# AdaLN/FFN adapter kernel on one core: two products with a narrow adapter matrix in two fp32r passes, hi and lo parts of the stationary operand side by side

## The chip, the cores and the metric

One Trainium2 chip, one of its cores. The metric is the device time of one execution in microseconds (us). TensorE's clock has two levels, 2.4 and 1.2 GHz; the profile gives the granted one as a share of full speed (1.0 or 0.5). Engines in the profile: PE is TensorE (PEld its weight loads), DVE VectorE, ACT ScalarE, POOL GpSimd, SP SyncE.

## What is computed

x has 8 batches of 256 tokens with 1024 features. The reference, cut to what matters:

```python
q     = quantize(x)             # 8 threshold groups: each element takes the step and zero point of its group
gates = softmax(top2(q @ router_w.T))                       # 4 experts
x1    = x + sum_e gates_e * (q @ A_e.T) @ B_e.T * 4         # rank 16 each, E*R0 = 64 in all
base  = x1 @ W.T + (x1 @ lora_A[label]) @ lora_B_w.T * 0.5  # rank 32, A chosen per batch
out   = x1 + base @ K + bias + (base @ A_eff.T) @ B_eff.T + (base @ A_s.T) @ B_s.T   # rank 32 each
```

## The kernel before

No product with W and then K is done per token. The kernel first forms K' = K + A_s.T B_s and P = W.T K' + I (1024 x 1024), and then out = x P + small terms. All products that need fp32 precision with large operands are done in fp32r passes: an operand is split into a hi part (a copy with rounding to fp32r, on ScalarE) and a lo part (the difference, on VectorE); three passes (hi hi, hi lo, lo hi) make one product. A matmul of plain fp32 operands shows as two records in the trace.

Stages, in order of time. (1) 0 to 36 us: loads; `aefft` (effective A of each batch), `k_update` and `k_add` form K' of the first half of the columns (`kst`, 8 tiles of 128x512); `kp_split` (ScalarE) and `kp_lo_part` (VectorE) split it into `kp_hi` and `kp_lo`. `keep_warm` issues matmuls whose result nobody reads. (2) `v_product(0)`: v = lora_B_w.T times K', 8 fp32 matmuls with the tile `bw` (lora_B_w tiled 4 times to 128 columns) as the stationary operand; `v_rows` copies 32 rows of it, times 0.5, into `tst`. (3) The T products: 8 fp32 matmuls (`gm` times `lb`, L828), which give the effective B of the batches; `rows_out` (ScalarE, L474) copies each into `tst`, which has two slots, and SyncE stores each slot to `t_dram` (L315). A slot is written again only when its store has landed (the wait on `t_stored`). (4) Steps 0 to 15 (`STEPS`), each one tile of P (128x512): steps 0 to 7 for the first half of K's columns, with the product u (L885, copied by ScalarE as `ust`, L523; the next u waits for that copy), steps 8 to 15 for the second half. Each is 24 passes (L902, L903, L906) of W's tile, split by `weight_hi` (ScalarE) and `weight_lo` (VectorE), with K'; its result is split into `p_hi` and `p_lo`. K' of the second half is made beside steps 0 to 7, split after step 7, and `v_product(1)` stands after step 7. (5) `bp`: the expert matrix B (`bet`, E*R0 = 64 columns, twice) times P: 48 passes, copied into the lower 64 rows of `tb` for both slots by `bp_out`. (6) 64 slots, 8 for each batch: x P in three passes (L949 to L951), `z_begin` and `z_end` (the adapter rows z, with `bu`), `close` (adapter rows times `tb`, L931), `out_tile` (bias, VectorE).

Beside all this ScalarE and VectorE quantize the batches: 64 groups `quant(c, g)` (batch c, group g), each two ScalarE passes over 2048 elements (L392, L403) and three VectorE ones (L576, L586, L593), and after the eighth group of a batch `finish` (L598), on which the `mid` products of TensorE (L837) wait. The order on every engine is written out by hand: the list `TAKEN` says how many groups stand in each slot; ScalarE is one slot ahead of VectorE. Every engine takes its instructions in order, and `wait_ge` holds the whole engine.

SyncE's order ahead of step 0: the 8 `alt` loads, the wait for kp_hi, kp_lo and v, the load of K's second half (`kst`, L311, 2 MB), then the four stores of `tst`.

## Time and profile before

| | us |
|---|---|
| median of 3 runs (lowest, highest) | 492.47 (491.3, 493.65) |
| span of the profiled execution, first to last instruction | 490.6 |
| its own time | not listed apart from the three runs; the lowest lies 0.7, the highest 3.05 above its span |
| TensorE busy | 471.1 |
| VectorE busy | 408.6 |
| ScalarE busy | 339.7 |
| mean granted clock of TensorE | 0.965 |

Times in the trace are us from the start of the span. A pair "start, us" is the start and the length of an instruction; a bracket behind it is the idle time of the engine just before and what ended it. A busy TensorE is not TensorE at its peak, since the ends of matmuls overlap: the pitch of two following records says what one costs.

### The profile page before, as it was taken

The numbers are of one execution on the slowest core, as the hardware profiler recorded it, in microseconds if no ns is written. First come the engines' busy times: TensorE is split into PE (matmuls) and PEld (weight loads), VectorE is DVE, ScalarE is ACT, GpSimd is POOL, SyncE is SP. The second block draws the span as 40 slices with busy tenths as digits, with TensorE's granted clock in tenths as the row PEclk, the third lists the DMA queues.
The fourth block names the chain that finished last, engine by engine and source line by source line (L and its number), as shares of the span: only waits on it lengthen the run. The fifth ranks groups of instructions, "written<-read, shape, count | busy, mean of one in ns | idle before, by whom it ended". The sixth has DMA issues, their size and how long they took to land.

```text
span 490.6 us, 5581 instructions
## 1 busy us (share of the span) xinstructions
PE 471.1 (96%) x2168; PEld 365.4 (74%) x2168; DVE 408.6 (83%) x411; ACT 339.7 (69%) x264; POOL 8.5 (2%) x12
## 2 busy tenths in 40 slices
PE   6989999999989999999999999999999989999796
PEld 5963888887758888787777777877787768767674
DVE  2289979779979989749899999999999994999402
ACT  3779987864978396676599596955977975583000
POOL 0000000001000000000000010000000000000000
PEclk9599999999999999999999999999999995999699
DMA  8975643212401527030523117104313130101102
GB/s 277 421 258 192 171 133 89 73 43 98 107 1 63 152 85 215 15 94 23 169 99 106 59 40 236 53 1 150 140 28 124 54 128 1 53 1 43 44 0 85
DMA packets 35499, 50.61 MB, mean 103 GB/s; under 512 B 26610, under 2 KB 26866, under 8 KB 33074
## 3 DMA queue, kind: packets, MB, share of 16 engines
q1 hardware_dynamic: 34322, 41.87, 26.6%
q0 software_dynamic: 1152, 8.39, 4.8%
q8 instruction: 17, 0.28, 0.2%
q14 instruction: 8, 0.07, 0.1%
HBM read 39.51 MB, written 10.49 MB: 102 GB/s over the span
## 4 chain that ended last, share of the span: by engine, by line
PE 62%; DVE 26%; issue 7%; DMA 2%; ACT 2%; SPq 0%; DVEq 0%; ACTq 0%
DVE val L593 12%; PE bank L949 7%; PE bank L951 7%; PE bank L950 7%; PE bank L837 6%; DVE val L576 5%; PE bank L906 5%; PE bank L902 5%; PE bank L903 4%; PE bank L931 3%; PE bank L863 3%; DVE inside L586 3%; PE bank L885 3%; PE bank L803 3%; DMA la<-la_in 2%
## 5 line engine op out<-in xcount | busy, mean ns | idle before, releaser
L403 ACT ACTIVATE val<-level,shift,small 128x2048 f32<-128x2048 int16 x64 | 133.8, 2090 | 22.5 <-DVE val L593 22.4
L593 DVE COPY_PREDICATED val<-inside,val 128x2048 f32<-128x2048 uint8 x56 | 142.1, 2538 | 0.3
L392 ACT ACTIVATE level<-xq,inv 128x2048 int16<-128x2048 f32 x64 | 127.9, 1998 | 2.2 <-DMA xq<-xt_in 1.4
L949 PE MATMUL bank<-p_hi,x_hi 128*128 128x512 f32 x256 | 113.1, 442 | 0.0
L951 PE MATMUL bank<-p_hi,x_lo 128*128 128x512 f32 x256 | 101.3, 396 | 0.0
L950 PE MATMUL bank<-p_lo,x_hi 128*128 128x512 f32 x256 | 101.2, 395 | 0.0
L576 DVE TENSOR_SCALAR val<-val,width,unshift 128x2048 f32<-128x2048 f32 x64 | 86.8, 1359 | 10.2 <-ACT val L403 10.0
L586 DVE TENSOR_SCALAR inside<-absx,thr 128x2048 uint8<-128x2048 f32 x56 | 72.1, 1297 | 6.1 <-ACT absx L384 6.1
L949 PEld LDWEIGHTS bank<-p_hi,x_hi 128*128 128x128 f32 x256 | 49.1, 192 | 18.9 <-issue 10.0
L950 PEld LDWEIGHTS bank<-p_lo,x_hi 128*128 128x128 f32 x256 | 48.9, 191 | 14.6 <-issue 5.8
L951 PEld LDWEIGHTS bank<-p_hi,x_lo 128*128 128x128 f32 x256 | 48.8, 191 | 10.8
L902 PE MATMUL bank<-kp_hi,w_hi 128*128 128x512 f32 x128 | 50.8, 397 | 1.8 <-DVE kp_lo L630 1.8
L906 PE MATMUL bank<-kp_hi,w_lo 128*128 128x512 f32 x128 | 50.3, 393 | 0.0
L903 PE MATMUL bank<-kp_lo,w_hi 128*128 128x512 f32 x128 | 49.9, 390 | 0.0
L837 PEld LDWEIGHTS bank<-ra,val 128*128 128x128 f32 x256 | 35.9, 226 | 7.2 <-DVE val L598 6.0
L837 PE MATMUL bank<-ra,val 128*128 128x68 f32 x256 | 36.1, 310 | 5.1 <-DVE val L598 5.1
L751 DVE TENSOR_TENSOR ost<-bank,bias 128x512 f32<-128x512 f32 x32 | 22.6, 713 | 17.7 <-PE bank L931 17.7
L931 PE MATMUL bank<-tb,zt 128*128 128x512 f32 x64 | 32.7, 599 | 0.0
L885 PE MATMUL bank<-aefft,wst 128*128 128x256 f32 x128 | 29.1, 380 | 2.3 <-ACT ust L523 2.3
L863 PE MATMUL bank<-xs,ub 128*64 128x256 f32 x128 | 29.3, 382 | 0.0
L885 PEld LDWEIGHTS bank<-aefft,wst 128*128 128x128 f32 x128 | 24.1, 190 | 6.9 <-issue 3.5
L902 PEld LDWEIGHTS bank<-kp_hi,w_hi 128*128 128x128 f32 x128 | 24.1, 188 | 6.4 <-issue 2.0
(86 smaller groups left out, 454.3 us busy)
## 6 DMA issues: line engine op xcount, KB each, us to landing
xq<-xt_in POOLq DMA_DIRECT2D x8, 1024.0 KB, 6.1
xs<-xt_in SPq DMA_DIRECT2D x8, 1024.0 KB, 4.9
out_t<-ost SPq DMA_DIRECT2D x16, 512.0 KB, 3.0
wst<-w_in SPq DMA_DIRECT2D x14, 512.0 KB, 3.6
la<-la_in SPq DMA_DIRECT2D x4, 512.0 KB, 10.6
kst<-k_in SPq DMA_DIRECT2D x4, 512.0 KB, 14.0
lb<-lb_in SPq DMA_DIRECT2D x1, 2048.0 KB, 19.9
kst<-k_in SPq DMA_DIRECT2D x1, 2048.0 KB, 7.8
```

The lines of the kernel that those rows point to most:

```text
L392: nc.scalar.activation(level[:, g % 2], xq[:, c % 2], ACT.Copy, scale=inv[:, g:g + 1]).then_inc(levels_made, 1)
L403: nc.scalar.activation(val[:, turn(c, g)], level[:, g % 2], ACT.Relu, bias=shift[:, g:g + 1], scale=par[:, 1, g:g + 1]).then_inc(raised, 1)
L576: nc.vector.tensor_scalar(v, v, width[:, g:g + 1], unshift[:, g:g + 1], ALU.min, ALU.add).then_inc(valued, 1)
L586: nc.vector.tensor_scalar(inside[:, g % 2], absx, thr[:, g - 1:g], None, ALU.is_le).then_inc(masked, 1)
L593: nc.vector.copy_predicated(val[:, acc(c)], inside[:, g % 2], val[:, turn(c, g)]).then_inc(merged, 1)
L837: last = mm(midbank[:, t * RT:(t + 1) * RT], val[:, acc(c), k, t * P:(t + 1) * P], ra[:, k], start=k == 0, stop=k == KT - 1)
L902: mm(obank[n % RING], w_hi[side(n)][:, o], kp_hi[:, o], start=o == 0, stop=False)
L903: mm(obank[n % RING], w_hi[side(n)][:, o], kp_lo[:, o], start=False, stop=False)
L906: last = mm(obank[n % RING], w_lo[side(n)][:, o], kp_hi[:, o], start=False, stop=o == KT - 1)
L949: mm(o, x_hi[:, s, k, at], p_hi[:, h, k], start=k == 0, stop=False)
L950: mm(o, x_hi[:, s, k, at], p_lo[:, h, k], start=False, stop=False)
L951: last = mm(o, x_lo[:, s, k, at], p_hi[:, h, k], start=False, stop=False)
```

## The change

Two products get fewer passes. For v, a new tile `bwp` holds for each of the 8 tiles of lora_B_w its lo part (32 columns) and its hi part (32 columns) side by side; one matmul with 96 columns of it (the last 32 belong to the next tile, and their rows are not read) gives lo and hi rows at once. Two passes, with `kp_hi` and `kp_lo`, replace the fp32 matmul; the lo rows are copied by ScalarE (`v_lo_rows`) and VectorE adds the hi rows (`v_add`). For bp, the tile `betp` holds lo and hi of `bet` (64 columns each) and two passes replace three; ScalarE copies the lo rows (`bp_lo_out`), VectorE adds the hi rows (`bp_add`), and ScalarE copies the sum into the second slot (`bp_copy`). `bw` now lies where `w_hi1` and `w_lo1` come later, so `weight_hi(1)` waits until `bw` has been read. `v_product` waits for `kp_lo` in place of `kst`; the first stands behind the fourth T product, the second behind step 8; on ScalarE the T rows stand ahead of groups 2 and 3. The closes of batch 0 begin two slots later.

```diff
@@ place
-    bw, bw_at = place("bw", [P, KT, P], F32)
-    bu, _ = place("bu", [P, 2, 2 * R], F32, bw_at)
+    bw, _ = place("bw", [P, KT, P], F32, xs_at, 2 * w_bytes)
+    bwp, _ = place("bwp", [P, KT * 2 * R + R], F32R)
+    bwp_k = bwp[:, 0:KT * 2 * R].rearrange("p (k c) -> p k c", k=KT)
+    bu, _ = place("bu", [P, 2, 2 * R], F32)
...
-    bet_hi, _ = place("bet_hi", [P, KT, 2 * ER], F32R, ost_at)
-    bet_lo, _ = place("bet_lo", [P, KT, 2 * ER], F32R, ost_at, KT * 2 * ER * 4)
+    betp, _ = place("betp", [P, KT, 2 * ER], F32R, ost_at)
@@ where the closes stand
-    CLOSE = [max(b * KT + 1, ZEND[b] + 1) for b in range(BATCH)]
+    CLOSE = [max(b * KT + (1 if b else 3), ZEND[b] + 1) for b in range(BATCH)]
@@ sync
             sp.wait_ge(kp_hi_made, KT)
             sp.wait_ge(kp_lo_made, KT)
-            sp.wait_ge(vfull, 1)
             sp.dma_start(kst, k_v[1]).then_inc(k2_in, 16)
@@ scalar
-            def v_rows(h):
+            def v_lo_rows(h):
                 act.wait_ge(vfull, h + 1)
-                nc.scalar.activation(tst[3 * R:4 * R, 0, h * HALF:(h + 1) * HALF], misc[3 * R:4 * R], ACT.Copy,
-                                     scale=LORA1).then_inc(v_made, 1)
+                if h:
+                    act.wait_ge(v_made, h)
+                nc.scalar.activation(tst[3 * R:4 * R, 1, 0:HALF], misc[0:R], ACT.Copy,
+                                     scale=LORA1).then_inc(v_lo_made, 1)
+            def bwp_hi():
+                act.wait_ge(bw_in, 16)
+                nc.scalar.activation(bwp_k[:, :, R:2 * R], bw[:, :, 0:R], ACT.Copy).then_inc(bwp_hi_made, 1)
...
-            def bp_out(s):
+            def bp_lo_out():
                 for h in range(HALVES):
                     act.wait_ge(bpfull, h + 1)
                     act.wait_ge(v_moved, 32)
-                    nc.scalar.activation(tb[2 * R:P, s, h * HALF:(h + 1) * HALF], sbank[h][ER:2 * ER], ACT.Copy).then_inc(bp_made, 1)
+                    nc.scalar.activation(tb[2 * R:P, 0, h * HALF:(h + 1) * HALF], sbank[h][0:ER], ACT.Copy).then_inc(bp_lo_made, 1)
+            def bp_copy():
+                act.wait_ge(bp_made, HALVES)
+                nc.scalar.activation(tb[2 * R:P, 1], tb[2 * R:P, 0], ACT.Copy).then_inc(bp_copied, 1)
...
             weight_hi(0)
+            bwp_hi()
             kp_split(0)
+            for n in range(RING):
+                rows_out(n)
             quant(*ORDER[2])
             act.wait_ge(consts_in, 16 * N_CONST)
             nc.scalar.activation(ident, ident_raw, ACT.Copy).then_inc(ident_made, 1)
+            act.wait_ge(cfull, 1)
+            act.wait_ge(bwp_made, 1)
             weight_hi(1)
+            v_lo_rows(0)
+            for n in range(RING, NG * HALVES):
+                rows_out(n)
             quant(*ORDER[3])
-            v_rows(0)
-            for n in range(NG * HALVES):
-                rows_out(n)
-                if n == NG - 1:
-                    quant(*ORDER[4])
+            quant(*ORDER[4])
...
-                if n == KT:
-                    v_rows(1)
+                if n == KT + 1:
+                    v_lo_rows(1)
...
-            bp_out(0)
+            bp_lo_out()
             bu_out(0)
...
-                if q == 1:
-                    bp_out(1)
+                if q == 2:
+                    bp_copy()
@@ vector
+            def v_add(h):
+                dve.wait_ge(v_lo_made, h + 1)
+                nc.vector.scalar_tensor_tensor(tst[3 * R:4 * R, 0, h * HALF:(h + 1) * HALF], misc[R:2 * R], LORA1,
+                                               tst[3 * R:4 * R, 1, 0:HALF], ALU.mult, ALU.add).then_inc(v_made, 1)
+            def bp_add(h):
+                dve.wait_ge(bp_lo_made, h + 1)
+                at = slice(h * HALF, (h + 1) * HALF)
+                nc.vector.tensor_tensor(tb[2 * R:P, 0, at], sbank[h][ER:2 * ER], tb[2 * R:P, 0, at], ALU.add).then_inc(bp_made, 1)
...
             weight_lo(0)
+            dve.wait_ge(bwp_hi_made, 1)
+            nc.vector.tensor_tensor(bwp_k[:, :, 0:R], bw[:, :, 0:R], bwp_k[:, :, R:2 * R].bitcast(F32), ALU.subtract).then_inc(bwp_made, 1)
             kp_lo_part(0)
...
             weight_lo(1)
+            v_add(0)
             quant(*ORDER[3])
@@ tensor
             def v_product(h):
-                pe.wait_ge(k_sum, (h + 1) * KT)
+                pe.wait_ge(kp_lo_made, (h + 1) * KT)
...
                 for o in range(KT):
-                    last = mm(misc, bw[:, o], kst[:, o], start=o == 0, stop=o == KT - 1)
+                    mm(misc[0:3 * R], bwp[:, 2 * R * o:2 * R * o + 3 * R], kp_hi[:, o], start=o == 0, stop=False)
+                    last = mm(misc[0:3 * R], bwp[:, 2 * R * o:2 * R * o + 3 * R], kp_lo[:, o], start=False, stop=o == KT - 1)
...
-            keep_warm(4)
-            v_product(0)
+            keep_warm(2)
             pe.wait_ge(lb_in, 16)
             for n in range(NG * HALVES):
+                if n == RING:
+                    v_product(0)
...
-                if n == KT - 1:
+                if n == KT:
                     v_product(1)
...
-                    mm(sbank[h], bet_hi[:, k], p_hi[:, h, k], start=o == 0, stop=False)
-                    mm(sbank[h], bet_hi[:, k], p_lo[:, h, k], start=False, stop=False)
-                    last = mm(sbank[h], bet_lo[:, k], p_hi[:, h, k], start=False, stop=o == KT - 1)
+                    mm(sbank[h], betp[:, k], p_hi[:, h, k], start=o == 0, stop=False)
+                    last = mm(sbank[h], betp[:, k], p_lo[:, h, k], start=False, stop=o == KT - 1)
...
-                        pe.wait_ge(bp_made, 2 * HALVES)
+                        pe.wait_ge(bp_made, HALVES)
```

ScalarE, from the split of K' (the kp_hi row) on, 36 to 53 us before the change. Before (`tst` 64x512 are the T rows, 32x512 is v; each pair `level`, `val` is a group):

```order
L428 ACTIVATE kp_hi<-kst 128x512 x8
L392 ACTIVATE level<-xq,inv 128x2048
L403 ACTIVATE val<-level,shift,small 128x2048
L498 ACTIVATE ident<-ident_raw 128x128
L421 ACTIVATE w_hi_97<-wst_101 128x1024
L392 ACTIVATE level<-xq,inv 128x2048
L403 ACTIVATE val<-level,shift,small 128x2048
L432 ACTIVATE tst<-bank 32x512
L474 ACTIVATE tst<-bank 64x512 x4
L392 ACTIVATE level<-xq,inv 128x2048
L403 ACTIVATE val<-level,shift,small 128x2048
L474 ACTIVATE tst<-bank 64x512 x4
```

and with the change:

```order
L430 ACTIVATE kp_hi<-kst 128x512 x8
L487 ACTIVATE tst<-bank 64x512 x4
L394 ACTIVATE level<-xq,inv 128x2048
L405 ACTIVATE val<-level,shift,small 128x2048
L514 ACTIVATE ident<-ident_raw 128x128
L423 ACTIVATE w_hi_97<-wst_101 128x1024
L437 ACTIVATE tst<-bank 32x512
L487 ACTIVATE tst<-bank 64x512 x4
L394 ACTIVATE level<-xq,inv 128x2048
L405 ACTIVATE val<-level,shift,small 128x2048
L394 ACTIVATE level<-xq,inv 128x2048
L405 ACTIVATE val<-level,shift,small 128x2048
```

The four T rows that stood behind group 3 are now the first thing after `kp_hi`, and v and the other four come ahead of groups 3, 4 and 5, which follow each other.

TensorE, between step 7 and step 8 (L902, L903, L906 or L941, L942, L945 are a step's passes, L847 and L886 the gated turn). Before:

```order
L903 MATMUL bank<-kp_lo,w_hi_97 128x512
L906 MATMUL bank<-kp_hi,w_lo_99 128x512
L795 MATMUL bank<-kst,bw 128x512 x8
L847 MATMUL bank<-ident,mg 128x128 x2
L902 MATMUL bank<-kp_hi,w_hi_97 128x512
L903 MATMUL bank<-kp_lo,w_hi_97 128x512
L905 MATMUL bank<-ident 128x128
```

and with the change, between steps 7 and 8, and then between steps 8 and 9:

```order
L942 MATMUL bank<-kp_lo,w_hi_97 128x512
L945 MATMUL bank<-kp_hi,w_lo_99 128x512
L886 MATMUL bank<-ident,mg 128x128 x2
L941 MATMUL bank<-kp_hi,w_hi_97 128x512
L942 MATMUL bank<-kp_lo,w_hi_97 128x512
```

```order
L942 MATMUL bank<-kp_lo,w_hi_97 128x512
L945 MATMUL bank<-kp_hi,w_lo_99 128x512
L832 MATMUL bank<-kp_hi,bwp 96x512
L833 MATMUL bank<-kp_lo,bwp 96x512
...
L832 MATMUL bank<-kp_hi,bwp 96x512
L833 MATMUL bank<-kp_lo,bwp 96x512
L941 MATMUL bank<-kp_hi,w_hi_96 128x512
L942 MATMUL bank<-kp_lo,w_hi_96 128x512
```

The product of the second half (L795) stood between step 7 and step 8; as 16 passes (L832, L833) it now stands behind step 8, and only the gated turn is left in its place.

## Rows read from the trace of the kernel before

**Rows 1.** The page, section 1: busy us (share of the span) xinstructions.

```profile
PE 471.1 (96%) x2168; PEld 365.4 (74%) x2168; DVE 408.6 (83%) x411; ACT 339.7 (69%) x264; POOL 8.5 (2%) x12
```

**Rows 2.** Waits of TensorE, waiting <- waited for: us in total, times, longest us.

```profile
PE bank L837 <- DVE val L598: 5.1, 2, 3.1
...
PE bank L885 <- ACT ust L523: 2.3, 1, 2.3
PE bank L902 <- DVE kp_lo L630: 1.8, 1, 1.8
```

**Rows 3.** The chain of waits ahead of step 8: start us, us, what.

```profile
142.03 0.70 DVE kp_lo L630
...
142.87 0.47 PE bank L902
```

**Rows 4.** TensorE in order of time (start us, us, instruction); last the chain at 191.

```profile
34.16 1.89 PE L773 MATMUL bank<-warm 128*128 128x256 f32 x8
35.89 7.03 PE L795 MATMUL bank<-kst,bw 128*128 128x512 f32 x16
42.85 7.21 PE L828 MATMUL bank<-lb,gmix 128*64 128x512 f32 x16
...
133.59 7.03 PE L795 MATMUL bank<-kst,bw 128*128 128x512 f32 x16
...
191.23 0.23 PE bank L922
```

**Rows 5.** VectorE in order of time, 36 to 75 us; [idle before <-releaser].

```profile
36.61 4.90 DVE L630 TENSOR_TENSOR kp_lo<-kst,kp_hi 128x512 fp32r<-128x512 f32 x8
...
47.74 1.35 DVE L576 TENSOR_SCALAR val<-val,width,unshift 128x2048 f32<-128x2048 f32 x1
...
73.67 1.23 DVE L617 TENSOR_TENSOR w_lo<-wst,w_hi 128x1024 fp32r<-128x1024 f32 x1 [2.68 <-ACT w_hi L421]
```

**Rows 6.** ScalarE in order of time, 36 to 64.5 us.

```profile
51.57 2.03 ACT L474 ACTIVATE tst<-bank 64x512 f32<-64x512 f32 x4
...
57.37 0.38 ACT L523 ACTIVATE ust<-bank 128x256 f32<-128x256 f32 x1
...
63.92 0.38 ACT L523 ACTIVATE ust<-bank 128x256 f32<-128x256 f32 x1 [1.34 <-PE bank L887]
```

**Rows 7.** SyncE: the load, the first stores; landing of load, first store, all four.

```profile
43.01 0.36 SPq L311 DMA_DIRECT2D kst<-k_in  x1
46.87 1.43 SPq L315 DMA_DIRECT2D t_dram<-tst  x2
...
DMA to landing us min/median/max: 7.8/7.8/7.8
...
DMA to landing us min/median/max: 4.6/4.6/4.6
...
DMA to landing us min/median/max: 2.8/3.7/4.6
```

**Rows 8.** Mid products of TensorE; two stretches, granted clock third from the end.

```profile
154.11 3.68 PE L837 MATMUL bank<-ra,val 128*128 128x68 f32 x32
...
405.22 6.89 PE L837 MATMUL bank<-ra,val 128*128 128x68 f32 x32 [2.02 <-DVE val L598]
...
414.00:416.00 2.00, 2.00 (x6) 1.55 (x6) 1.86 (x6) 2.00 (x2) 0.00 (x0) 0.57 0.00 0
466.00:468.00 2.00, 2.00 (x8) 1.60 (x7) 0.92 (x5) 0.00 (x0) 0.00 (x0) 0.77 0.00 0
```

**Rows 9.** In order of time after step 15: ScalarE's bu, TensorE's gated matmul.

```profile
203.22 0.22 ACT L459 ACTIVATE bu<-bank 64x64 f32<-64x64 f32 x1
...
206.39 0.64 PE L870 MATMUL bank<-zt,bu 64*64 64x256 f32 x2
```

**Rows 10.** The chain at 240 us, and VectorE's next idle time.

```profile
240.40 0.57 PE bank L870 x2
...
245.31 1.35 DVE L576 TENSOR_SCALAR val<-val,width,unshift 128x2048 f32<-128x2048 f32 x1 [2.20 <-ACT val L403]
```

More of the change, by code:

```diff
@@ L192, in build @@
     bufull, bu_made = sem("bufull"), sem("bu_made")
+    bwp_padded, bwp_hi_made, bwp_made = sem("bwp_padded"), sem("bwp_hi_made"), sem("bwp_made")
+    v_lo_made, bp_lo_made, bp_copied = sem("v_lo_made"), sem("bp_lo_made"), sem("bp_copied")
     zfull, zt_made = sem("zfull"), sem("zt_made")
@@ L530, in _ @@
                     act.wait_ge(bet_in, 16)
-                    nc.scalar.activation(bet_hi, bet, ACT.Copy).then_inc(bet_hi_made, 1)
+                    nc.scalar.activation(betp, bet, ACT.Copy).then_inc(bet_hi_made, 1)
                 if n in OUT:
@@ L633, in _ @@
             nc.vector.memset(warm, 1.0).then_inc(warm_made, 1)
+            nc.vector.memset(bwp[:, KT * 2 * R:].bitcast(F32), 0.0).then_inc(bwp_padded, 1)
             dve.wait_ge(small_in, 16)
@@ L732, in _ @@
                     p_out(n - 1)
+                if n == KT + 1:
+                    v_add(1)
                 if n == STEPS - 1:
                     dve.wait_ge(bet_hi_made, 1)
-                    nc.vector.tensor_tensor(bet_lo, bet, bet_hi.bitcast(F32), ALU.subtract).then_inc(bet_lo_made, 1)
+                    nc.vector.tensor_tensor(betp[:, :, 0:ER], bet[:, :, 0:ER], betp[:, :, ER:2 * ER].bitcast(F32), ALU.subtract).then_inc(bet_lo_made, 1)
                 if n == KT - 1:
@@ L760, in _ @@
                         quant(c, g)
+                    if b == 0 and j == 0:
+                        for h in range(HALVES):
+                            bp_add(h)
                     if b + 1 < BATCH and j - 1 in XAT:
@@ L788, in v_product @@
             def v_product(h):
-                pe.wait_ge(k_sum, (h + 1) * KT)
+                pe.wait_ge(kp_lo_made, (h + 1) * KT)
                 if h == 0:
-                    pe.wait_ge(bw_in, 16)
+                    pe.wait_ge(bwp_padded, 1)
+                    pe.wait_ge(bwp_made, 1)
                 else:
@@ L960, in _ @@
                     pe.wait_ge(v_moved, 32)
-                    pe.wait_ge(bp_made, HALVES * min(c + 1, 2))
+                    pe.wait_ge(bp_made, HALVES)
+                    if c:
+                        pe.wait_ge(bp_copied, 1)
                     for m in range(c * TILES, min((c + 1) * TILES, (q + 1) // 2)):
```

## Prediction

> **What bounds the kernel now.** I read the page first: TensorE is busy 96% of the span [rows 1]. That looks like a kernel in which any matmul taken out comes off the time. The waits of TensorE say where this fails [rows 2]: few, and for the same two engines. The chain of waits shows what they mean: until about 60 us it is TensorE, up to 142.87 us it runs through VectorE and ScalarE (quantization groups, splits of W and K'), and the first matmul of step 8 follows kp_lo, not TensorE [rows 3]. From there TensorE does not wait until 403 us, and VectorE is full in turn from 245 us on. So a matmul saved before 142 us is paid out only if it lets ScalarE and VectorE start earlier; one saved or added between 143 and 240 us counts whole.
>
> **B times K', first half.** Removed: 8 fp32 matmuls (two records each) from 35.89 to 42.85 us, 6.96 us. Added: 16 fp32r passes. Those of 512 columns follow each other by 0.23 us [rows 4]; I take the same for a stationary tile of 96 columns, so 3.65 us, 3.3 less. Two of the four warming matmuls go, 1.73/4 x 2 = 0.87 us. TensorE would be 4.2 us ahead, but the product now reads kp_lo, and so must wait for it. Before, kp_lo ended at 41.43 us [rows 5]; VectorE first makes the lo half of bwp (256 elements, some 0.35 us, estimated from 0.6 for 512), so 41.8. TensorE does four T products first (35.0 to 38.6 us at 0.89 each), idles 3.2 us, and multiplies from 41.9 to 45.7.
>
> **The order on ScalarE** matters more. Before, it had no idle time from 35.6 to 62.6 us, and only 1.34 us then; four T rows and a group take 5.80 us (51.57 to 57.37), 1.9 and 3.9 [rows 6]. Now the first four T rows come directly after kp_hi: they end with the T products, at 39.2. Then group 2 (3.9), ident, W hi: 44.3. It waits for v until 45.8 and copies it (46.3). The next T row overwrites tst slot 0, and must wait until its store to DRAM has landed. That store is now issued behind the 2 MB load of K's second half, 0.4 us after it and not 3.9 us. Before, the load was issued at 43.01 and took 7.8 us, to 50.8; the store, issued at 46.87, took 4.6 us, to 51.5, just behind it; the later stores, with nothing ahead, took 2.8 at the least [rows 7]. I take it that the store lands behind the load: issue 41.9, load landed 49.7, store 50.4. ScalarE thus goes on at 50.4, four rows (1.9) to 52.3, then three groups in a row (3.9 each) to 64.0, where the copy of u stood at 57.37.
>
> The Trainium skill ("DMA: Bandwidth & Descriptors", section "Queues, rings and completion order") says that completion isn't first in, first out for an issuing engine; by that the small store need not wait for the big load, and the sum below would be 3.3 us smaller. The rows' 4.6 against 2.8 us speaks for waiting; it is a rival below.
>
> **What that does to VectorE.** It was full from 36 to 62.9 us, group 3 starting at 47.74 [rows 5]. The value of group 3 now comes at 52.3 + 3.9 = 56.2. Three groups (4.8, 5.0, 4.8) end at 70.9; k_add 0.6, W lo 1.15, p_lo 0.6, a group 4.9, k_add 0.6 end at 78.7, against 73.67 for W lo of the third tile: 5.1 late, with the old idle time of 2.68 used up. The other way round, TensorE's step 1 waits for u: u copied at 64.3, TensorE idle since 58.9 (step 0 as long as before). After 2.02 and 3.11 us of idling the granted clock fell to 0.5 (1.2 GHz); after 2.28 and 1.80 it stayed at 1.0 [rows 2, 8]. After 5.4 us I expect the fall, 1.6 us lost (below): u of step 1 is ready at 70.0, its copies end at 70.8, four ScalarE passes (7.9) and W hi (1.0) bring the split to 79.7, 6.0 late. From 81 to 143 us both engines take turns (a value waits for a merge, W hi for the value, W lo for W hi) with no slack that could take it in, so step 8 starts **6.0 us** later. TensorE, late by 6 there too, had 2.28 us to spare before step 7 and doesn't add to it.
>
> **B times K', second half.** It stood where TensorE waited anyway: 133.59 to 140.46 us, then 0.6 of gated turn and 1.80 us of idle [rows 2, 3]. It moves behind step 8, since it needs kp_lo. What was free there costs 16 x 0.23 = **3.65 us** where nothing else covers it. In its old place stands a gap of some 8.7 us (142.87 - 133.59 - 0.6). The clock falls in it. It came back at 415.7 and 466.9 us (worked out from the mean clocks 0.57 and 0.77), 3.6 and 2.8 us after 512-column work had begun at 412.1 and 464.1 [rows 8]; at half speed that loses 1.4 to 1.8: **1.6 us**. If it stays low as long as after 405.2 us, where 6.9 us of short matmuls came first, 5.
>
> **B times P.** 48 passes become 32: 16 x 0.23 = 3.65 us off, at 191 to 202 us, on the path. The gated part then waits for the copy of bu on ScalarE: it comes 12.2 us after step 15's end (191.1 + 12.2 = 203.4), TensorE used to come to it at 206.39, now 3.65 earlier at 202.7 [rows 9]. 0.7 is given back: **-2.9 us**. The bounds are -3.65, if the copy comes in time, and -2.5, if batch 1 waits for its x lo as well.
>
> Costed at nothing: bwp hi (0.38 us on ScalarE, before a wait of 2.30), the two adds of v and the two of bp (0.6 each; the first two of them in VectorE's idle time, those of bp under its wait of 5.48 at 207 to 212 us), the copy of bp (0.95, on ScalarE, whose wait for TensorE at 240 us covers it), and the closes two slots later (as many, same order). If that cover went, they would cost up to 2 us together. SyncE's later wait for v is not behind anything urgent: W's tile follows only when W lo is split, at the same time.
>
> Up to TensorE's step at 240.40 us, which releases VectorE at 245.31 after 2.20 us of idling [rows 10], the sum is 6.0 + 3.65 + 1.6 - 2.9 = **+8.3 us**; both engines are full after it, so it reaches the end. The span goes from 490.6 to 498.9. The median of the three runs, 492.47, lies 1.9 above the profiled span: **500.8 us** (+1.7%). Half a per cent, 2.5 us, is about what a measurement of this kernel can tell from no change.
>
> **Rivals.** (a) The small store lands early: after 2.8 us, at 45.2. ScalarE is then held by the T products only, ends four rows at 49.7, and VectorE is late by 2.7 instead: +5.0, 497.5 us. For it, the page's rule; against it, the store's 4.6 us. 14%.
> (b) **The late clock falls go away.** At 405.2 and 457.2 us the clock fell, the first time after only 2.02 us of idling, less than the 2.28 that did nothing. Each costs: the mid product took 6.89 us against 3.68, 3.2 more, and 1.4 to 1.8 behind it. A shifted kernel may miss both: 3.2 + 5.0 = 8.2 back, 492.6 us; one alone, 497. 9%.
> (c) **TensorE sets the time after all**, and the result is faster. The place is the start of step 8: if kp_lo is there when TensorE comes, or VectorE's chain shrinks with TensorE's, then 3.3 + 0.9 + 3.3 + 3.6 = 11.1 come off less 0.7: 482 us. It decides as soon as VectorE and ScalarE have more slack before 143 us than the 1.80 and 2.28 us waits show. For it, 96% busy; against it, the chain. 8%.
> (d) The delay before step 8 is absorbed (the T rows are no hold-up): 3.65 + 1.6 - 2.9 = +2.4, 494.9 us. 9%.
> (e) Clocks cost more: both at 5 us, +12, 504 us. 8%.
>
> **How the numbers follow.** Forecast 52%, (a) 14, (b) 9, (c) 8, (d) 9, (e) 8. The range from 494.5 to 504.5 leaves out (c), most of (b) and a part of (e). Slower by over 0.5% (above 494.9): forecast, (a), (e), half of (b) and (d), 83%; same 8%; faster 9%.
>
> **What would show it.** Right: ScalarE waits some 4 us before its fifth T row, for the store; TensorE idles for u of step 1; step 8 starts near 149 us after a gap over 8 us, with the clock at 0.5; the second B product follows step 8 and takes 3.65; bp takes 7.3. Wrong: step 8 before 144 us, or no gap before it.

## The result, and the profile after

| | before | with the change |
|---|---|---|
| median of 4 runs (lowest, highest), us | 491.88 (491.13, 493.65) | 500.7 (499.4, 501.07) |
| ratio, 95% interval | | 1.0167 (1.0137 to 1.0196) |
| span of the profiled execution, us | 490.6 | 498.9 |
| mean granted clock of TensorE | 0.965 | 0.945 |

The change makes the kernel 1.7% slower. The page of the changed kernel, busy times and the granted clock in 40 slices of 12.5 us:

```profile
PE 467.9 (94%) x2148; PEld 365.3 (73%) x2148; DVE 411.3 (82%) x417; ACT 341.0 (68%) x264; POOL 11.9 (2%) x12
...
PEclk9588979999897999999999999999999997999699
```

TensorE is busy for 3.2 us less than in [rows 1], though its clock is lower. It waits longer. Its waits, us in total, times, longest:

```profile
PE bank L941 <- DVE kp_lo L657: 7.1, 1, 7.1
PE bank L924 <- ACT ust L540: 6.2, 2, 4.0
PE bank L876 <- DVE val L615: 4.6, 2, 2.5
...
PE bank L832 <- DVE kp_lo L657: 3.1, 1, 3.1
...
PE bank L909 <- ACT bu L468: 0.3, 1, 0.3
```

The wait of 1.8 us ahead of step 8 [rows 2] is now 7.1, that for u of step 1 is new, 4.0, and so are the 3.1 ahead of the first B product and the 0.3 for bu. The first link is in the chain of waits from 42 us on (start, us, what), and in ScalarE's order of time:

```profile
42.15 0.36 SPq L313
42.51 0.05 issue
42.56 8.05 DMA t_dram<-tst
...
50.69 0.57 ACT tst L487
```

```profile
47.65 0.58 ACT L437 ACTIVATE tst<-bank 32x512 f32<-32x512 f32 x1 [3.01 <-PE bank L833]
50.69 2.04 ACT L487 ACTIVATE tst<-bank 64x512 f32<-64x512 f32 x4 [2.45 <-DMA t_dram<-tst]
...
64.57 0.36 ACT L540 ACTIVATE ust<-bank 128x256 f32<-128x256 f32 x1
...
71.62 0.38 ACT L540 ACTIVATE ust<-bank 128x256 f32<-128x256 f32 x1 [1.86 <-PE bank L926]
```

The store issued just behind the 2 MB load of `kst` (L313) holds `tst` for 8.05 us, the T rows end at 52.7, and the copy of u that stood at 57.37 [rows 6] stands at 64.57. TensorE in order of time, at the places the prediction named:

```profile
65.08 6.06 PE L924 MATMUL bank<-aefft,wst 128*128 128x256 f32 x16 [3.97 <-ACT ust L540]
...
131.52 5.27 PE L924 MATMUL bank<-aefft,wst 128*128 128x256 f32 x16 [2.24 <-ACT ust L540]
...
142.77 0.61 PE L886 MATMUL bank<-ident,mg 128*128 128x128 f32 x4
150.48 0.77 PE L941 MATMUL bank<-kp_hi,w_hi 128*128 128x512 f32 x1 [7.10 <-DVE kp_lo L657]
...
152.11 0.63 PE L941 MATMUL bank<-kp_hi,w_hi 128*128 128x512 f32 x1
...
158.37 0.39 PE L832 MATMUL bank<-kp_hi,bwp 128*96 128x512 f32 x1
...
162.02 0.39 PE L941 MATMUL bank<-kp_hi,w_hi 128*128 128x512 f32 x1
```

Step 8 starts at 150.48, 7.6 us later than at 142.87 [rows 3]. It takes 7.89 us (150.48 to 158.37) where a step at full clock takes 5.68 (e3, below). The second B product takes 3.65 us, to 162.02. The granted clock shows why step 8 is long (last row), and that the first B product (first row) and the product u of step 1 (second row) were struck too (stretch, length, busy, ..., clock third from the end):

```profile
42.00:46.00 4.00, 3.87 (x10) 2.61 (x11) 2.54 (x4) 2.65 (x3) 0.00 (x0) 0.57 0.74 221
...
66.00:70.00 4.00, 4.00 (x11) 3.14 (x10) 4.00 (x4) 3.76 (x3) 1.84 (x1) 0.52 0.25 42
...
152.00:156.00 4.00, 4.00 (x12) 3.09 (x12) 4.00 (x7) 3.95 (x6) 0.00 (x0) 0.60 0.00 0
```

A fourth fall lies at 131.52 us, after 2.24 us of idling: u of step 7 takes 5.27 us, where the kernel before took 3.69. This is why TensorE comes to the gap ahead of step 8 only at 142.77. The row of before:

```profile
123.88 3.69 PE L885 MATMUL bank<-aefft,wst 128*128 128x256 f32 x16 [2.28 <-ACT ust L523]
```

VectorE's **mark**, the value of a group behind its last longer wait, stands at 255.50 us, 10.2 later than at 245.31 [rows 10]; and the first of the late mid products (TensorE) looks better than that of [rows 8]:

```profile
255.50 1.35 DVE L593 TENSOR_SCALAR val<-val,width,unshift 128x2048 f32<-128x2048 f32 x1 [0.67 <-ACT val L405]
```

```profile
415.40 4.73 PE L876 MATMUL bank<-ra,val 128*128 128x68 f32 x32 [2.01 <-DVE val L615]
```

So 10.2 us are lost by 255 us and the span is only 8.3 longer: 1.9 came back later.

### The profile page after: what moved, and what is told of

Its sections match the earlier page's. It is cut to its first block, busy times and chain, and to the rows that moved or that the text cites. A ratio compares the mean times of both kernels' runs of the same rounds, so it can differ in the third digit from the quotient of the medians.

```text
span 498.9 us, 5547 instructions
## 1 busy us (share of the span) xinstructions
PE 467.9 (94%) x2148; PEld 365.3 (73%) x2148; DVE 411.3 (82%) x417; ACT 341.0 (68%) x264; POOL 11.9 (2%) x12
## 4 chain that ended last, share of the span: by engine, by line
PE 55%; DVE 27%; issue 8%; ACT 5%; DMA 4%; SPq 0%; DVEq 0%; ACTq 0%
DVE val L610 11%; PE bank L987 7%; PE bank L989 7%; PE bank L988 7%; PE bank L876 5%; DVE val L593 5%; PE bank L941 4%; PE bank L945 4%; PE bank L942 4%; PE bank L969 3%; DVE inside L603 3%; PE bank L902 3%; PE bank L924 3%; PE bank L841 3%; ACT val L405 2%
## 5 line engine op out<-in xcount | busy, mean ns | idle before, releaser
L941 PE MATMUL bank<-kp_hi,w_hi 128*128 128x512 f32 x128 | 51.8, 405 | 7.1 <-DVE kp_lo L657 7.1
L945 PE MATMUL bank<-kp_hi,w_lo 128*128 128x512 f32 x128 | 51.1, 399 | 0.0
L942 PE MATMUL bank<-kp_lo,w_hi 128*128 128x512 f32 x128 | 50.7, 396 | 0.0
L924 PE MATMUL bank<-aefft,wst 128*128 128x256 f32 x128 | 33.1, 417 | 6.2 <-ACT ust L540 6.2
L876 PEld LDWEIGHTS bank<-ra,val 128*128 128x128 f32 x256 | 33.2, 211 | 6.6 <-DVE val L615 5.4
L876 PE MATMUL bank<-ra,val 128*128 128x68 f32 x256 | 33.4, 295 | 4.6 <-DVE val L615 4.6
L924 PEld LDWEIGHTS bank<-aefft,wst 128*128 128x128 f32 x128 | 26.8, 212 | 12.3 <-issue 7.8
L941 PEld LDWEIGHTS bank<-kp_hi,w_hi 128*128 128x128 f32 x128 | 24.6, 192 | 11.8 <-issue 7.3
L634 DVE TENSOR_TENSOR w_lo<-wst,w_hi 128x1024 fp32r<-128x1024 f32 x14 | 17.1, 1223 | 15.1 <-ACT w_hi L423 15.1
## 6 DMA issues: line engine op xcount, KB each, us to landing
la<-la_in SPq DMA_DIRECT2D x4, 512.0 KB, 10.2
```

Source lines behind the costliest of these rows:

```text
L876: last = mm(midbank[:, t * RT:(t + 1) * RT], val[:, acc(c), k, t * P:(t + 1) * P], ra[:, k], start=k == 0, stop=k == KT - 1)
L924: mm(ubank, wst[n % 2][:, o], aefft[:, o], start=o == 0, stop=False)
L941: mm(obank[n % RING], w_hi[side(n)][:, o], kp_hi[:, o], start=o == 0, stop=False)
L945: last = mm(obank[n % RING], w_lo[side(n)][:, o], kp_hi[:, o], start=False, stop=o == KT - 1)
```

## Experiments

Twelve kernels, each with its median and the interval of its ratio to the kernel before, which was measured beside it on the same chip. There were four series, on four chips: e1, e4, e5 and e6 (the kernel before had 491.78 us), e2, e3 and e7 (491.2), e8 to e11 (492.87), and e12 (491.39). Between series the ratios say more than the medians.

| run | what it is | median, us | ratio to before (95%) |
|---|---|---|---|
| e1 | change, store ahead of the load | 500.17 | 1.0156 (1.0122, 1.019) |
| e2 | e1, TensorE kept busy ahead of the first B product | 498.54 | 1.0159 (1.0128, 1.0189) |
| e3 | change, TensorE kept busy ahead of step 8 | 502.01 | 1.0219 (1.0179, 1.026) |
| e4 | change, second half of B times K' as before | 496.53 | 1.0086 (1.0052, 1.0121) |
| e5 | change, first half and its orders as before | 493.61 | 1.004 (1.0021, 1.0059) |
| e6 | before, only B times P new | 487.88 | 0.9924 (0.9898, 0.9949) |
| e7 | e6, fillers ahead of the late mid products | 481.92 | 0.9813 (0.9789, 0.9837) |
| e8 | change, same fillers | 495.81 | 1.0073 (1.0045, 1.0101) |
| e9 | before, same fillers | 485.11 | 0.9861 (0.983, 0.9892) |
| e10 | e3 with same fillers | 496.59 | 1.0085 (1.0051, 1.0119) |
| e11 | e5 with same fillers | 488.24 | 0.9915 (0.9889, 0.9942) |
| e12 | e11, TensorE kept busy ahead of step 8 | 487.28 | 0.992 (0.9879, 0.9961) |

### The start: the store, and the clock in the first gap

SyncE's order in e1:

```diff
-            sp.wait_ge(kp_hi_made, KT)
-            sp.wait_ge(kp_lo_made, KT)
-            sp.dma_start(kst, k_v[1]).then_inc(k2_in, 16)
-
             for g in range(NG):
+                if g == 2:
+                    sp.wait_ge(kp_hi_made, KT)
+                    sp.wait_ge(kp_lo_made, KT)
+                    sp.dma_start(kst, k_v[1]).then_inc(k2_in, 16)
                 sp.wait_ge(t_made, 2 * (g + 1))
```

> The change, but SyncE issues the stores of tst slots 0 and 1 ahead of the 2 MB load of K's second half. My theory: the wait of ScalarE for the landing of the store (2.45 us ahead of the fifth T row in the changed kernel) goes, but v comes at 47.5 us only (its product ran partly at 0.5 of the clock) and the last four T rows follow TensorE's T products, so ScalarE leaves the rows at about 51.6 and not 52.6 us: 1.0 us sooner, 499.7 us. Rival, the store alone holds ScalarE back: rows end at 49.7, the chain is 3 us sooner, about 497.6 us. Third: the order of transfers doesn't matter, 500.7 us.

500.17 us, half a microsecond under the change. The four stores of `tst`, of which the first two no longer stand behind the load, landed fast:

```profile
DMA to landing us min/median/max: 2.8/2.8/2.9
```

ScalarE in order of time shows the store's wait gone and something else in its place:

```profile
49.39 0.58 ACT L437 ACTIVATE tst<-bank 32x512 f32<-32x512 f32 x1 [3.02 <-PE bank L833]
50.39 0.59 ACT L487 ACTIVATE tst<-bank 64x512 f32<-64x512 f32 x1 [0.42 <-PE bank L867]
51.25 0.59 ACT L487 ACTIVATE tst<-bank 64x512 f32<-64x512 f32 x1 [0.27 <-PE bank L867]
```

This run began 1.7 us later than the change's (kp_hi 35.16 against 33.43), so its rows end 0.9 us earlier by the same start. ScalarE is now held by TensorE: v comes late because the B product ran at half clock, and every T row waits for its T product. At the end of the T rows the store's wait is thus worth 0.9 of its 2.45 us. Behind that it is worth more. TensorE:

```profile
65.91 5.24 PE L924 MATMUL bank<-aefft,wst 128*128 128x256 f32 x16 [3.06 <-ACT ust L540]
```

It idles 3.06 us here and not 3.97, the low clock is shorter (5.24 us against 6.06), and step 8 starts at 150.60 us, by the same start 1.6 sooner than in the change. The medians say 0.5, but the four runs of e1 spread over 2.7 us: the store is worth 0.5 to 1.6 us, and these runs do not tell which.

e2 puts seven matmuls that nobody reads ahead of the product of e1, so that TensorE doesn't idle there:

```diff
                 if n == RING:
+                    pe.wait_ge(k_sum, KT)
+                    for _ in range(7):
+                        mm(misc[:, 0:WARM], aefft[:, 0, 0:P], aefft[:, 0], start=True, stop=True)
                     v_product(0)
```

> The stores first, as in the first experiment, and 7 matmuls whose result nobody reads in TensorE's gap of 3.14 us ahead of the first half of B times K'. My theory: the product then runs at clock 1.0 (3.65 and not 5.4 us) and v, the T rows and ScalarE's groups come 1.7 us sooner than with the stores alone; the gap at step 1 stays near 3 us. With the stores alone 0.9 us was gained at the end of the T rows; here 2.6 in all, 498.1 us, and up to 0.8 to 2.4 less if the clock doesn't fall at step 1. Rival, the clock there doesn't matter since VectorE is late anyway: 500.2 us as with the stores alone.

498.54 us, near the 498.1 expected. The T rows end at 50.6 and u of step 1 starts at 63.02 (ScalarE and TensorE in order of time):

```profile
50.09 0.59 ACT L487 ACTIVATE tst<-bank 64x512 f32<-64x512 f32 x1 [0.27 <-PE bank L870]
```

```profile
63.02 5.18 PE L927 MATMUL bank<-aefft,wst 128*128 128x256 f32 x16 [3.05 <-ACT ust L540]
```

Step 8 starts at 147.71 us; kp_hi's last group stood at 33.88, so by the same start this is 1.6 us sooner than in e1 and 3.2 sooner than in the change. The medians put both holds together at 2.2 us of the change's 8.8, but e1 and e2 come from different series, and by their ratios to the kernel before (1.0156 and 1.0159) e2 is no faster than e1. What the trace shows is where the time goes; how much of it is left at the end is known only roughly. What remains of the delay would be the order itself, the three groups in a row ahead of u: no run puts the groups alone back in their old places, so this is argued and not shown.

### The halves of the change

e4 gives the second half of B times K' back its fp32 matmuls and its place behind step 7 (two tiles are placed elsewhere for it):

```diff
-                if n == KT:
+                if n == KT - 1:
                     v_product(1)
@@ v_product
+                if h:
+                    for o in range(KT):
+                        last = mm(misc, bw[:, o], kst[:, o], start=o == 0, stop=o == KT - 1)
+                    last.then_inc(vfull, 1)
+                    return
```

> The change, but the second half of B times K' is done as before: 8 fp32 matmuls behind step 7, v copied by ScalarE alone. TensorE does 3.3 us more work than in the change. My theory: the gap ahead of step 8 is filled, step 8 starts at 150.5 us as in the change, but with the clock at 1.0 (2.2 us back) and nothing between steps 8 and 9 (3.65 us back): step 15 ends at 198.7 instead of 204.6 us, 494.8 us in all (unless the late clock falls move). Rival, TensorE's work sets the time: 504.0 us.

496.53 us: 4.2 us faster than the change, while TensorE does twice the work for this product, but 1.7 above the 494.8 expected. In order of time:

```profile
141.67 7.07 PE L829 MATMUL bank<-kst,bw 128*128 128x512 f32 x16
...
151.00 0.47 PE L948 MATMUL bank<-kp_hi,w_hi 128*128 128x512 f32 x1 [1.82 <-DVE kp_lo L659]
...
153.08 0.63 PE L948 MATMUL bank<-kp_hi,w_hi 128*128 128x512 f32 x1
...
158.28 0.39 PE L948 MATMUL bank<-kp_hi,w_hi 128*128 128x512 f32 x1
```

The old product fills the gap and the wait is 1.82 us again as in [rows 2], but step 8 still starts at 151.00. So the product is not what makes step 8 late. The expectation failed in the clock: it fell all the same, one microsecond into the step (a pass at 153.08 takes 0.63 us, at full clock 0.39), and step 8 took 7.28 us (151.00 to 158.28), only 0.6 less than in the change, where 2.2 had been expected. What e4 shows is the price of the product's place, 3.65 us, and hardly anything of the clock's.

e5 does the reverse: first half as fp32 ahead of the T products, ScalarE's T rows behind group 3 and SyncE's load behind v, as before. (Its second half uses 64 columns of `bwp`, placed elsewhere, in place of 96.)

```diff
-            for n in range(RING):
-                rows_out(n)
             quant(*ORDER[2])
...
+            quant(*ORDER[3])
+            act.wait_ge(vfull, 1)
+            nc.scalar.activation(tst[3 * R:4 * R, 0, 0:HALF], misc[3 * R:4 * R], ACT.Copy,
+                                 scale=LORA1).then_inc(v_made, 1)
+            for n in range(NG * HALVES):
+                rows_out(n)
+                if n == NG - 1:
+                    quant(*ORDER[4])
```

> The change, but the first half of B times K' and the order of ScalarE and SyncE around it are as before; second half and B times P as in the change (64 columns of bwp instead of 96). My theory: the delay before step 8 comes all from the first half, so step 8 starts at 142.9 us; then 2.2 (clock) and 3.65 (product behind step 8) are added and 3.2 (B times P) taken off: 2.7 us over the kernel before, 494.6 us. Rival, the first half costs nothing in the end and the second all: 500.7 us. Rival, TensorE's work sets the time: about 485 us.

493.61 us, 7.1 faster than the change (6.2 by the ratios; 494.6 expected), and step 8 is back in its place, with the gap and the fallen clock still there:

```profile
142.78 0.77 PE L945 MATMUL bank<-kp_hi,w_hi 128*128 128x512 f32 x1 [7.00 <-DVE kp_lo L657]
```

e6 is the kernel before with B times P alone as in the change (betp, two passes, the adds and the copy of bp, the closes two slots later):

```diff
-                    mm(sbank[h], bet_hi[:, k], p_hi[:, h, k], start=o == 0, stop=False)
-                    mm(sbank[h], bet_hi[:, k], p_lo[:, h, k], start=False, stop=False)
-                    last = mm(sbank[h], bet_lo[:, k], p_hi[:, h, k], start=False, stop=o == KT - 1)
+                    mm(sbank[h], betp[:, k], p_hi[:, h, k], start=o == 0, stop=False)
+                    last = mm(sbank[h], betp[:, k], p_lo[:, h, k], start=False, stop=o == KT - 1)
```

> The kernel before with only the part on B times P changed (two passes for three, adds and copy as in the change). My theory: 16 passes less stand on the path; TensorE's gated matmul comes 3.2 us sooner, step 8 at 142.9 us as before: 488.7 us. Rival, the full 3.65: 488.2. Rival, ScalarE's and VectorE's added copies and adds, or the copy of bu, take it all back: 491.9 us.

487.88 us (488.7 expected): this part of the change alone makes the kernel faster. It does so although the clock fell in its step 8, after a wait of 1.81 us, and not in that of the kernel before, after 1.80 (141.96 to 149.22 us, 7.26 against 5.67).

### Keeping the clock up ahead of step 8, a miss

```diff
+                if n == KT:
+                    pe.wait_ge(k_sum, 2 * KT)
+                    for _ in range(15):
+                        mm(misc[:, 0:WARM], aefft[:, 0, 0:P], aefft[:, 0], start=True, stop=True)
                 pe.wait_ge(w_lo_made, load_of(n) + 1)
```

> The change, with 15 matmuls whose result nobody reads (6.4 us) in TensorE's gap ahead of step 8. My theory: the clock stays at 1.0, the gap is filled but not passed, step 8 takes 5.7 and not 7.9 us: 2.2 us off, 498.5 us. Rival, the low clock there costs nothing in the end because ScalarE or VectorE is behind: 500.7 us.

502.01 us, where 498.5 had been expected, and 1.3 above the change, from which it can't be told (the intervals of the ratios overlap). Yet the gap and the step came out as expected (TensorE in order of time; 152.11 to 157.79 is 5.68 us for step 8):

```profile
152.11 0.47 PE L945 MATMUL bank<-kp_hi,w_hi 128*128 128x512 f32 x1 [0.56 <-DVE kp_lo L657]
...
157.79 0.39 PE L832 MATMUL bank<-kp_hi,bwp 128*96 128x512 f32 x1
...
415.74 6.55 PE L876 MATMUL bank<-ra,val 128*128 128x68 f32 x32 [2.15 <-DVE val L615]
```

The last row has the other half: this run got the dear clock fall in batch 6, 6.55 us where the change's profile had 4.73, and it began 1.2 us later (first B product at 43.32 against 42.13). Comparing a few microseconds across such falls says little, so the next runs take the falls away.

### The late clock falls taken out of both kernels

Unread matmuls stand ahead of the wait of the mid products of batches 6 and 7 (the wait for `mgt_made` moves ahead of them):

```diff
+                if c >= 6:
+                    pe.wait_ge(bias_in, 16)
+                    for _ in range(LATE[c - 6]):       # LATE = (4, 10)
+                        mm(midbank[:, 0:WARM], bias[:, 0:P], bias[:, 0:WARM], start=True, stop=True)
                 pe.wait_ge(q_made, c + 1)
```

> The kernel with only B times P changed, and 4 and 10 matmuls whose result nobody reads ahead of the mid products of the last two batches, where TensorE waits 2.1 and 4.7 us for VectorE. My theory: the clock no longer falls there; the last mid product takes 3.7 and not 7.1 us, and 1.4 us come back behind it: 4.8 us off 487.9, 483.1 us, and less spread between runs. Rival, the low clock there isn't on the path: 487.9 us.

481.92 us (483.1 expected), the fastest of all, 1.9% under the kernel before, with 0.4 us between its lowest and highest run. Both mid products take 3.79 us after waits of half a microsecond:

```profile
402.06 3.79 PE L854 MATMUL bank<-ra,val 128*128 128x68 f32 x32 [0.45 <-DVE val L603]
...
451.00 3.79 PE L854 MATMUL bank<-ra,val 128*128 128x68 f32 x32 [0.55 <-DVE val L603]
```

The same fillers in the changed kernel, in the kernel before, and in e5:

> The changed kernel with 4 and 10 unread matmuls ahead of the mid products of batches 6 and 7 (they compute nothing of the output; they only keep TensorE from idling there). The run of the kernel before with the new B times P and the same fillers had 481.9 us, with VectorE's mark (the first group after its wait at 240 to 256 us) at 242.00 us. In the changed kernel the same mark stands at 255.50, 13.5 later. Theory (everything the change costs is paid before that mark, and the rest of the differences lies in the late clock falls): 481.9 + 13.5 = 495.4 us. Rival (the change also costs something in the 64 slots after the mark): 497 us or more.

> The kernel before, nothing of the change, with the same 4 and 10 unread matmuls ahead of the mid products of batches 6 and 7. Its VectorE mark stands at 245.31 us, 3.3 later than in the run of 481.9 us. Theory: 481.9 + 3.3 = 485.2 us, so that the change as a whole costs 10.2 us and not the 8.8 that the plain comparison shows, and B times P alone is worth 3.3. Rival (the fillers are worth 5.96 us here as there, and the rest of B times P's gain is real): 491.5 - 6.0 = 485.5 by that too; a time under 483.5 would say that B times P is worth less than 2 us and that the plain comparison lent it a late clock fall of the kernel before.

> The changed kernel with the first half of B times K' and the orders of ScalarE and SyncE ahead of step 0 as before, and the same fillers ahead of the late mid products. What is left of the change is the second half behind step 8 and the new B times P. The run without fillers had the VectorE mark at 248.53 us. Theory: 481.9 + 6.5 = 488.4 us, so that the delay ahead of step 8 by itself is 495.4 - 488.4 = 7.0 us. Rival (the delay is worth only the 6.0 of the prediction or less): 489.4 us or more.

495.81, 485.11 and 488.24 us, each within half a microsecond of what the mark of VectorE foretold (495.4, 485.2, 488.4). So close an agreement has luck in it: the runs of e8 spread over 4.1 us, those of e9 over 2.8 and those of e11 over 3.3, and the marks are those of single profiled runs without the fillers. The marks of e8 and e9, first the change's:

```profile
255.58 1.35 DVE L594 TENSOR_SCALAR val<-val,width,unshift 128x2048 f32<-128x2048 f32 x1 [0.75 <-ACT val L406]
```

```profile
246.28 1.35 DVE L577 TENSOR_SCALAR val<-val,width,unshift 128x2048 f32<-128x2048 f32 x1 [2.18 <-ACT val L404]
```

With the late falls out, the change costs 10.7 us by the medians of e8 and e9, one series (10.4 by the ratios), where the plain comparison has 8.8. The two profiled runs lie closer together, 9.3 us at the mark and 9.4 in the span (493.4 and 484.0). A cost above 8.8 is likely, then, but it is not clear of the noise. By the medians it splits: the delay ahead of step 8 is e8 less e11, 7.6 us; the second half behind step 8 with its clock is e11 less e7, 6.3; B times P is e7 less e9, -3.2. The last two cross series; by the ratios to before they are 5.0 (1.02%) and -2.4 (0.48%), and the first is 7.8.

e10 adds the fillers ahead of step 8 to e8:

> The changed kernel with the same fillers ahead of the late mid products and 15 unread matmuls in the gap ahead of step 8. The earlier run with the 15 alone was 1.3 us slower than the change instead of 2.2 faster, though its step 8 took 5.68 us and not 7.89. Theory (that run had the dearer late clock fall, 6.55 us for a mid product against 4.73, and began 1.2 us later): with the late falls gone the step is worth 1.0 to 2.2 us, since of the 2.2 gained 0.8 goes back in the wait for the copy of bu (1.1 us there against 0.32): 493.2 to 494.4 us where the same kernel without the 15 has 495.4. Rival (the 15 matmuls cost something elsewhere, as much as they give): no faster than the kernel without them.

496.59 us, runs from 492.5 to 499.0: not to be told from e8. The profiled spans (492.4 and 493.4) differ by 1.0 us as the theory says, but this says nothing for it: e10's run began 1.5 us sooner (first B product at 41.51 against 43.00). e12 asks the same where the start is as before:

> The kernel of the run of 488.24 us (first half of B times K' and its orders as before, second half behind step 8, new B times P, fillers ahead of the late mid products) with the 15 unread matmuls in the gap ahead of step 8 added. There step 8 started after 8.68 us of idling and took 7.36 us in the profile (8.45 in the run without the late fillers), and 5.68 us is what a step takes at full clock, so 1.7 to 2.8 us lie in the clock. In the changed kernel the same 15 gave 1.0 us in the profiles and nothing that the medians could show (496.59 against 495.81, runs from 492.5 to 499.0). Theory (the clock ahead of step 8 costs 1.0 to 2.2 us at the end, a part being given back in the wait for the copy of bu; the noise of the earlier pair came from the start of the kernel, which is as before here): 486.0 to 487.2 us. Rival (the 15 matmuls give nothing at the end, because the copy of bu or a later wait takes all of it): 488.2 us or more.

487.28 us, 1.0 under e11 and just outside the range expected; with runs from 484.8 to 490.9 it can't be told from e11 (486.6 to 489.9). So none of e3, e10 and e12 shows at the end the 1.7 to 2.8 us that step 8 itself gets back. The eight runs fall in two groups: four from 484.8 to 486.0 us with a mean clock of 0.982, four from 488.5 to 490.9 with 0.975 or 0.976. The profiled one is of the second group. TensorE in order of time, and the clock of two stretches (third from the end):

```profile
208.88 0.64 PE L918 MATMUL bank<-zt,bu 64*64 64x256 f32 x2 [1.77 <-ACT bu L470]
...
210.56 0.63 PE L1000 MATMUL bank<-p_hi,x_hi 128*128 128x512 f32 x1
```

```profile
210.00:212.00 2.00, 2.00 (x6) 1.51 (x6) 1.97 (x3) 0.00 (x0) 0.00 (x0) 0.50 1.05 336
212.00:214.00 2.00, 2.00 (x8) 1.58 (x7) 1.97 (x3) 1.74 (x2) 0.00 (x0) 0.68 0.47 74
```

TensorE, no longer late from step 8, comes earlier to the wait for the copy of bu: it waits 1.77 us there, where e11 waited 0.55, and the clock falls behind it. What the fillers gave is spent at the next wait; the profile's mark is 0.4 us later than e11's (249.35 against 248.98), although step 9 had begun 2.4 earlier (152.79 against 155.21; 0.7 of that was an earlier kp_lo). The group of 0.982 would then be the runs in which the clock held: 2.8 us or so under e11. That group has no trace, so this is inferred from the mean clocks, and there is a second candidate: e12's profile has a fall at u of step 7 as well (5.38 us from 124.46, where e11 took 3.69). Whether e10's spread has the same cause (it waited 1.39 us for bu and kept its clock in the profile) was not seen.

## Why the prediction was right

The forecast was 500.8 us (range 494.5 to 504.5), the result 500.7, and the chain of events is the one described. Not all sizes were right: several were too small, and one late gain, not in the sum, made up for them. The base moved too: the forecast adds 8.3 us to 492.47, while the median of four runs is 491.88 and the measured difference 8.8.

- **What bounds it.** Right. TensorE lost 3.2 us of busy time and the kernel got slower; e4 and e5 show each half paying by where it puts its waits.
- **First half, no effect of the matmuls saved.** Right in kind: kp_lo released the product at 42.13 (41.9 predicted), after 3.14 us of idling (3.2). Wrong in that a fall of the clock in this gap was left out: "from 41.9 to 45.7" was 42.13 to 47.5, 5.4 us against 3.65. e2 shows in the trace that it matters: without it step 8 starts 1.6 us sooner by the same start.
- **The store behind the load.** Right: landed at 50.6 (50.4), ScalarE on at 50.69. Its own price is small, since e1, without the wait, is 0.5 us faster by the medians and 1.6 sooner at step 8 by the trace: the late v and the T products stand right behind it. Rival (a) was wrong on both counts, for the store did not land early, and one that isn't behind the load buys 0.5 to 1.6 us and not 3.3. The Trainium skill ("DMA: Bandwidth & Descriptors", section "Queues, rings and completion order") says that completion is not first in, first out. The same section says that each DMA engine takes its descriptors in ring order, so the prediction drew too much from the first sentence: it is no reason for the small store to pass the load. The traces agree: the store took 8.05 us behind the load, and 2.8 to 2.9 without a load ahead (e1).
- **"Step 8 starts 6.0 us later"** was 7.6. Of the missing 1.6, half lies in the copy of u (64.9 at its end, 64.3 predicted, and u's product begun at 65.08), half in u of step 1 at the low clock: its product and copy took 6.5 us from 65.08 to the copy at 71.62, where 5.7 were taken. TensorE idled 3.97 us ahead of it and not 5.4, since it was late itself. From there on the chain passed the delay on unchanged, as said: VectorE's W lo stood at 81.38, 7.7 later than in [rows 5]. The measured price of the whole is 7.1 us (e5) and 7.6 (e8 less e11), by the ratios 6.2 and 7.8. This term was the one most under-sized.
- **Second half, +3.65 and +1.6.** 3.65 is right to the digit (158.37 to 162.02). The clock took 2.2 in this profile (7.89 less 5.68), and between 1.7 (e11: 7.36) and 2.8 (e5: 8.45) in others. Together e11 less e7 has 5.0 to 6.3, 5.25 predicted. That the clock's part is paid at the end was not shown by taking it away: e3, e10 and e12 did so in step 8, and no median fell beyond the noise. The gap was 7.1 us and not 8.7, since u of step 7 ran at the low clock (5.27 us against 3.69) and TensorE came to the gap that much later; e1, e2 and e8, without that fall, have 8.66, 8.67 and 8.74.
- **B times P, -2.9.** Between 204.55 and 211.90 us stand 7.35 us where 10.97 stood, 3.62 off; the wait for bu gives back 0.32 (0.7 predicted). That makes -3.3 (e7's mark, 242.00, lies as much ahead of 245.31), and e7 less e9 has -2.4 to -3.2. e6 against before shows 3.7 by its ratio, a part of which is a milder late fall (3.79 us against 6.89 for batch 6).
- **The sum.** Up to the mark it was 10.2 and not 8.3. "Both engines are full after it, so it reaches the end" holds when the clock is kept up (e8 less e9: 10.7), but in the plain kernels rival (b) came true by a part: the fall of batch 6 came later in the mid product, 4.73 us against 6.89, 2.2 back. That the total is right to 0.1 us is thus luck: about 2 us of it are two errors of opposite sign.
- **Rivals (c), (d).** Step 8 did not start before 144 us, and nothing absorbed the delay (e5). (e) overstated the clock: no fall ahead of step 8 cost over 2.8. Its sum does not come out either: both falls at 5 us make 6.0 + 3.4 + 3.65 + 5 - 2.9, some +15 and not +12.

## What to carry to other kernels

A product that uses fewer passes but needs a later input can cost more than it saves: ask first whether the old one stood in a gap, and what waits on its new input. Before sizing a change of some microseconds, take the unrelated clock falls out of both kernels with a few unread matmuls ahead of the waits; here this changed 8.8 us to 10.7 by the medians, and was itself worth 5 to 8 us. Look at the start of each profiled run as well: those here began up to 1.7 us apart, as much as many of the effects sought. And filling one gap can lengthen the next: with the 15 matmuls ahead of step 8 the wait for bu was 1.1 to 1.8 us, without them 0.3 to 0.6. The best version (e7, 481.92 us) keeps only the part of the change that lies on TensorE's own path, B times P, and holds the clock through batches 6 and 7.

## What was not expected of the hardware

- The clock can fall after a short wait and need not, and the same wait ahead of the same work goes either way. Ahead of step 8, 1.80 to 1.82 us of idling were followed by the fall in e4 and e6 (7.28 and 7.26 us for the step) and by none in the kernel before, e7 and e9 (5.64 to 5.67). Ahead of u of step 7, it fell after 2.24 to 2.36 us in the change, e3, e5, e10 and e12, and held after 2.28 to 2.43 in the other nine traces. The prediction's reading of [rows 2, 8], no fall after 1.80 and 2.28, was one profile's.
- After 3.13 to 3.15 us ahead of the first B product it fell in the change, e1, e3, e4 and e8, from the first pass (e8) to the sixth (e1) on, and held in e10 (the T rows then waited 4.3 us for the store, and nothing was gained). After 1.77 us ahead of the bu matmul it fell in e12, after 1.39 in e10 it did not.
- The same wait before the same mid product ended in 4.73, 6.55 or 6.89 us of short matmuls (2.01, 2.15, 2.02 us of idling), and in 3.79 where the fall came only behind them or not at all. They are a part of the run-to-run spread: the kernel before spans 3 to 5 us in each series, with these waits filled 2.8 (e9), and e7 0.4. They are not all of it, since e8 still spans 4.1.
- A stationary tile of 96 columns follows at the same pitch as one of 128, 0.23 us for 512 columns, and so does one of 64 (e5), so the columns nobody reads cost nothing.
